# B and C of a scan step from one narrow matmul, spread over the partitions through DRAM

## What is computed

```python
dbc = xs @ x_proj_w.T                       # 16 columns for dt, 16 for B, 16 for C
dt = softplus(dbc[..., :16] @ dt_proj_w.T + dt_proj_b)
Bm = dbc[..., 16:32]
Cm = dbc[..., 32:]
dA = exp(dt[..., None] * A)
dBu = dt[..., None] * Bm[:, :, None, :] * xs[..., None]
hs = scan(h = dA * h + dBu)                 # along the tokens
y = einsum('blds,bls->bld', hs, Cm) + xs * Dvec
y = (y * silu(z)) @ out_proj_w.T
```

## Time and profile before

| | |
|---|---|
| median of 3 runs | 4836.43 us |
| the profiled execution's own time | 4842.17 us |
| its span, first to last instruction | 4840.4 us |
| mean granted TensorE clock | 0.957 of full speed |
| busy, of the span | PE 88%, DVE 83%, POOL 81%, ACT 68% |
| DMA | 623 MB, 129 GB/s on average |

### The profile page before, as it was taken

How to read it: one execution, slowest core, us unless ns; L and a number is a source line. 1 busy time by engine, 2 the same in 40 slices (tenths; PEclk the granted TensorE clock), 3 DMA queues, 4 the chain that set the end, 5 groups by cost and what they waited for, 6 DMA issues and landing times.

```text
span 4840.4 us, 69756 instructions
## 1 busy us (share of the span) xinstructions
PE 4236.6 (88%) x21206; PEld 1773.4 (37%) x21206; DVE 4002.3 (83%) x5617; ACT 3314.4 (68%) x5382; POOL 3939.5 (81%) x5162
## 2 busy tenths in 40 slices
PE   3578788999999999999989999999999989898897
PEld 1233333333333343434333434343333333333332
DVE  2268889888988888988898989888989898988872
ACT  1356566777777777777767776777777777676665
POOL 1268888888888888888888888888888889898873
PEclk9688899999999999999999999999999999999998
DMA  2366665656555665666656655666665665554430
GB/s 68 79 141 158 145 141 131 143 135 140 136 137 137 140 138 133 138 139 138 141 131 146 141 136 134 139 139 137 140 138 136 145 140 138 132 125 115 95 78 5
DMA packets 255529, 623.06 MB, mean 129 GB/s; under 512 B 105268, under 2 KB 170676, under 8 KB 255028
## 3 DMA queue, kind: packets, MB, share of 16 engines
q1 hardware_dynamic: 255156, 618.60, 55.8%
HBM read 540.85 MB, written 77.65 MB: 128 GB/s over the span
## 4 chain that ended last, share of the span: by engine, by line
POOL 35%; PE 24%; DVE 17%; issue 11%; DMA 7%; ACT 4%; SPq 0%; DVEq 0%; POOLq 0%; ACTq 0%
POOL hc L1156 14%; DVE hs L1011 7%; PE ps L676 5%; DMA dtb<-dt_scratch 5%; DVE ps L1001 4%; PE ps L740 3%; POOL sp L1169 2%; PE ps L689 2%; DVE tmpd L1070 2%; POOL h L1196 2%; POOL yw L1256 2%; PE ps L717 2%; POOL sp L1177 2%; PE ps L800 2%; PE ps L811 2%
## 5 line engine op out<-in xcount | busy, mean ns | idle before, releaser
L1156 POOL TENSOR_TENSOR hc<-hs,cb 128x448 f32<-128x448 f32 x1792 | 2025.6, 1137 | 460.5 <-DVE hs L1011 315.9
L1011 DVE TENSOR_TENSOR_SCAN hs<-dtb,state,ps 128x448 f32<-128x448 f32 x1536 | 1754.7, 1142 | 84.8 <-issue 0.7
L1001 DVE TENSOR_TENSOR ps<-ps,bb 128x448 f32<-128x448 f32 x1792 | 1099.1, 613 | 439.7 <-PE ps L676 437.9
L848 ACT ACTIVATE dtb<-dtb,decay 128x448 f32<-128x448 f32 x1792 | 1092.0, 658 | 156.0 <-DMA dtb<-dt_scratch 154.1
L676 PE MATMUL ps<-dux,pick 128*128 128x448 bf16 x3584 | 1038.1, 371 | 128.7 <-DVE hs L1011 117.1
L890 ACT ACTIVATE hg<-ps,be 128x448 f32<-128x448 f32 x896 | 523.8, 630 | 405.2 <-PE ps L740 404.6
L676 PE MATMUL ps<-duz,pick 128*128 128x448 bf16 x1792 | 642.5, 359 | 0.0
L676 PEld LDWEIGHTS ps<-dux,pick 128*128 128x128 bf16 x3584 | 283.7, 101 | 831.4 <-issue 432.1
L740 PE MATMUL ps<-xn,we 64*128 64x448 f32 x1792 | 564.5, 592 | 7.9 <-ACT hg L890 5.3
L879 ACT ACTIVATE rz<-ps,bnb 128x448 f32<-128x448 f32 x448 | 280.8, 627 | 271.4 <-PE ps L724 271.0
L689 PE MATMUL ps<-hc,gather 128*32 128x448 f32 x3584 | 451.3, 573 | 0.0
(11 more groups left out here) (171 smaller groups left out, 6319.3 us busy)
## 6 DMA issues: line engine op xcount, KB each, us to landing
dtb<-dt_scratch SPq DMA_DIRECT2D x448, 896.0 KB, 6.7
slab<-h_scratch SPq DMA_DIRECT2D x168, 290.0 KB, 8.3
dt_scratch<-sp SPq DMA_DIRECT2D x112, 224.0 KB, 2.0
h_scratch<-h2p SPq DMA_DIRECT2D x168, 112.0 KB
h<-h_scratch SPq DMA_DIRECT2D x56, 336.0 KB, 4.3
h_scratch<-h1s SPq DMA_DIRECT2D x56, 232.0 KB, 2.2
xw<-xn_scratch SPq DMA_DIRECT2D x112, 112.8 KB, 2.7
xw<-xn_scratch SPq DMA_DIRECT2D x112, 112.5 KB, 3.7
```

The costliest lines, as they stand in the source:

```text
L848: A.activation(a, a, ACT.Exp, scale=decay[k % 2][:, i:i + 1]).then_inc(a_ok, 1)
L1001: V.tensor_tensor(bank, bank, bb[:, k % 2, :], ALU.mult).then_inc(bu_ok, 1)
L1011: V.tensor_tensor_scan(rev(hs[:, n % RH, :], d), rev(dtb[i // 4][:, i % 4, :], d), rev(bank, d), state[:, d, i:i + 1] if k % STEPS >= 2 el ...
L1156: P_.tensor_tensor(hc[:, n % 8, :], hs[:, n % RH, :], cb[:, k % 2, :], ALU.mult).then_inc(hc_ok, 1)
```

## The change

Each step makes B and C together in one matmul with the plain weights of 32 columns, into 32 partitions (`bc` at slot -15). ACT copies 32 partitions (`copy_bc`). SP writes them to DRAM (`put_bc`, 56 KB) and reads them back twice with each row 8 times (`spread_b` and `spread_c`, 224 KB each), into the same double-buffered `bb` and `cb`. `weigh_b` and `by_c` now wait for these DMAs. `wbb` and `wcc` and the four DVE copies of the prologue that made them are gone. `AHEAD` goes from 6 to 5, and all place tables are new.

```diff
-AHEAD = 6
+AHEAD = 5
...
-STEP_AT = {'fetch_xw': -27, 'x': -20, 'silu_u': -20, 'dt': -17, 'soft_in': -17, 'bb': -12, 'copy_bb': -11, 'cc': -10, 'copy_cc': -9, 'z': -5, 'soft_le': -17, 'soft_ym': -17, 'soft_log': -15, 'soft_dt': -14, 'part0': -14, 'part1': -12, 'part2': -3, 'put_dt': -10, 'spread0': -5, 'spread1': -2, 'spread2': -2, 'spread3': 1, 'skip': 8, 'gather0': 9, 'gather1': 13, 'gather2': 15, 'gather3': 19, 'gate': 19, 'out_proj': 21, 'add_out': 21}
-UP_AT = (0, 0, 1, 1, 2, 2, 3, 3, 8, 8, 9, 9, 10, 10, 11, 11)
-DOWN_AT = (5, 7, 12, 15)
-PAIR_AT = (3, 7, 12, 14)
-THIRD_AT = (0, 0, 1, 2, 2, 3, 5, 5, 6, 7, 7, 10, 10, 11, 12, 13)
-FOLD_AT = (3, 5, 6, 8, 9, 11, 14, 14, 14)
-A_AT = {'cut': -11, 'second': -11, 'put0': -9, 'rem1': -9, 'split1': -7, 'put1': -6, 'rem2': -8, 'split2': -6, 'put2': -4, 'arrange': -1, 'x_in': 12, 'paths': 15, 'mean': 16, 'square': 18, 'var': 18, 'power': 18, 'scaled': 21, 'normed': 22, 'norm_T': 25, 'keep_xn': 26}
-F_AT = {'fetch': 1, 'x_T': 3, 'paths_in': 5, 'rows': 8}
-E_AT = {'mean': 1, 'square': 2, 'var': 2, 'power': 4, 'normed': 4, 'tokens_T': 9, 'logits': 10, 'compare': 12, 'places': 13, 'lead': 13, 'ask': 16, 'weigh': 19, 'share': 19, 'weights': 21, 'weight_parts': 21, 'parts': 25, 'fold': 49, 'out': 53}
+STEP_AT = {'fetch_xw': -22, 'x': -20, 'silu_u': -20, 'dt': -17, 'soft_in': -17, 'bc': -15, 'copy_bc': -14, 'put_bc': -11, 'spread_b': -6, 'spread_c': 0, 'z': -5, 'soft_le': -17, 'soft_ym': -16, 'soft_log': -14, 'soft_dt': -13, 'part0': -9, 'part1': -3, 'part2': -3, 'put_dt': -10, 'spread0': -6, 'spread1': -4, 'spread2': 0, 'spread3': 1, 'skip': 7, 'gather0': 8, 'gather1': 13, 'gather2': 15, 'gather3': 19, 'gate': 19, 'out_proj': 20, 'add_out': 20}
+UP_AT = (0, 0, 1, 1, 2, 2, 3, 3, 8, 8, 9, 9, 10, 10, 10, 10)
+DOWN_AT = (4, 7, 12, 15)
+PAIR_AT = (4, 6, 11, 12)
+THIRD_AT = (0, 0, 1, 2, 2, 3, 5, 5, 6, 7, 7, 9, 11, 12, 13, 13)
+FOLD_AT = (4, 6, 7, 8, 10, 10, 13, 14, 14)
+A_AT = {'cut': -16, 'second': -10, 'put0': -9, 'rem1': -9, 'split1': -7, 'put1': -5, 'rem2': -7, 'split2': -5, 'put2': -3, 'arrange': 0, 'x_in': 8, 'paths': 14, 'mean': 16, 'square': 18, 'var': 18, 'power': 19, 'scaled': 21, 'normed': 23, 'norm_T': 26, 'keep_xn': 27}
+F_AT = {'fetch': 1, 'x_T': 5, 'paths_in': 6, 'rows': 8}
+E_AT = {'mean': 0, 'square': 2, 'var': 2, 'power': 4, 'normed': 4, 'tokens_T': 9, 'logits': 10, 'compare': 12, 'places': 13, 'lead': 13, 'ask': 16, 'weigh': 18, 'share': 19, 'weights': 20, 'weight_parts': 22, 'parts': 25, 'fold': 47, 'out': 48}
...
+                def put_bc(kk):
+                    sp_.wait_ge(m_act, by_act("bc", kk))
+                    sp_.dma_start(bc_dram[kk % 2], bc[:, :]).then_inc(bc_out, 16)
+
+                def spread_bc(kk, half):
+                    sp_.wait_ge(bc_out, 16 * (kk + 1))
+                    if kk >= 2:
+                        sp_.wait_ge(hc_ok if half else bu_ok, DS * (kk - 1))
+                    out, landed = ((bb, bb_in), (cb, cb_in))[half]
+                    src = bc_dram[kk % 2, DS * half:DS * half + DS, :]
+                    sp_.dma_start(out[:, kk % 2, :], src.unsqueeze(1).to_broadcast([DS, 8, CH]))\
+                       .then_inc(landed[kk % 2], 16)
...
-                    if what == "bb":
-                        last = MM(out[:, 0:CH], wbb[of % 2][:, :], u[:, of % 2, :], start=True, stop=True)
-                    elif what == "cc":
-                        last = MM(out[:, 0:CH], wcc[of % 2][:, :], u[:, of % 2, :], start=True, stop=True)
+                    if what == "bc":
+                        last = MM(out[0:2 * DS, 0:CH], wbc[of % 2][:, :], u[:, of % 2, :], start=True, stop=True)
...
+                def copy_bc(kk):
+                    act.wait_ge(m_ps, misc_made("bc", kk))
+                    after(bc_out, 16 * kk)
+                    A.activation(bc[:, :], ps[MB][0:2 * DS, 0:CH], ACT.Copy).then_inc(m_act, 1)
...
-                        dve.wait_ge(m_act, by_act("bb", k))
+                        dve.wait_ge(bb_in[k % 2], 16 * (k // 2 + 1))
...
-                        pool.wait_ge(m_act, by_act("cc", k))
+                        pool.wait_ge(cb_in[k % 2], 16 * (k // 2 + 1))
```

More of the change, by code:

```diff
@@ L116, in build @@
         wdt = [sb(f"wdt{d}", [DI, DI]) for d in range(2)]
-        wbb = [sb(f"wbb{d}", [DI, 128]) for d in range(2)]
-        wcc = [sb(f"wcc{d}", [DI, 128]) for d in range(2)]
+        wbc = [sb(f"wbc{d}", [DI, 2 * DS]) for d in range(2)]
         skip = [sb(f"skip{d}", [DI, 128]) for d in range(2)]
@@ L143, in build @@
         dtb = [sb(f"dtb{j}", [128, 4, CH]) for j in range(4)]
+        bc = sb("bc", [2 * DS, CH])
         bb = sb("bb", [128, 2, CH])
@@ L193, in build @@
         rows = [early[:, 1408 + 128 * d:1536 + 128 * d] for d in range(2)]
-        wbc = [early[:, 1664 + 2 * DS * d:1664 + 2 * DS * d + 2 * DS] for d in range(2)]
         bnv = early[:, 1728:1810]
@@ L295, in _ @@
                                   dvec[d][:, 3:3 + DS].unsqueeze(2).to_broadcast([DI, DS, 8])).then_inc(s_rows, 1)
-                    for out, at in ((wbb[d], 0), (wcc[d], DS)):
-                        then(V.tensor_copy(out[:, :].rearrange("p (s e) -> p s e", e=8),
-                                           wbc[d][:, at:at + DS].unsqueeze(2).to_broadcast([DI, DS, 8])))
                     then(V.tensor_copy(wz[d][:, :].rearrange("p (q r) -> p q r", q=4),
@@ L378, in build @@
         xw_in = [sem("xw_in0"), sem("xw_in1")]
+        bc_out, bb_in, cb_in = sem("bc_out"), [sem("bb_in0"), sem("bb_in1")], [sem("cb_in0"), sem("cb_in1")]
         dtb_in = [sem(f"dtb_in{j}") for j in range(4)]
@@ L506, in build @@
         for k in range(LAST):
-            MISC += [(DS * k + STEP_AT[what], what, k) for what in ("x", "dt", "bb", "cc")]
+            MISC += [(DS * k + STEP_AT[what], what, k) for what in ("x", "dt", "bc")]
         for what in ("tokens_T", "logits", "fold"):
@@ L627, in _ @@
                         fetch_xw(kk)
+                    for kk in steps_at(n, "put_bc"):
+                        put_bc(kk)
+                    for kk in steps_at(n, "spread_b"):
+                        spread_bc(kk, 0)
+                    for kk in steps_at(n, "spread_c"):
+                        spread_bc(kk, 1)
                     for kk in steps_at(n, "put_dt"):
@@ L915, in soft_in @@
                     A.activation(sp[:, 2, :], sp[:, 0, :], ACT.Ln, bias=1.0).then_inc(dt_l, 1)
[L917 to L920, removed]
-                    A.activation(bb[:, kk % 2, :], ps[MB][:, 0:CH], ACT.Copy).then_inc(m_act, 1)
-                def copy_cc(kk):
-                    act.wait_ge(m_ps, misc_made("cc", kk))
-                    if kk >= 2:
-                        act.wait_ge(hc_ok, DS * (kk - 1))
-                    A.activation(cb[:, kk % 2, :], ps[MB][:, 0:CH], ACT.Copy).then_inc(m_act, 1)
+                def copy_bc(kk):
+                    act.wait_ge(m_ps, misc_made("bc", kk))
+                    after(bc_out, 16 * kk)
+                    A.activation(bc[:, :], ps[MB][0:2 * DS, 0:CH], ACT.Copy).then_inc(m_act, 1)
                 def split_h2(it, a):
@@ L973, in _ @@
                         weigh(it)
-                    for kk in steps_at(n, "copy_bb"):
-                        copy_bb(kk)
-                    for kk in steps_at(n, "copy_cc"):
-                        copy_cc(kk)
+                    for kk in steps_at(n, "copy_bc"):
+                        copy_bc(kk)
                     for kk in steps_at(n, "soft_in"):
```

1 line of the change is left out of this document (added).

## The result

The changed kernel takes 5140.06 us (median of 4 runs, 5122.29 to 5154.96), against 4834.59 us before on the same chip: a ratio of 1.0627 [1.0598, 1.0656], 305 us **slower**. 4782 us were forecast, with a range up to 4890. The worst rival stood at 4900. The profiled run took 5155 us, 15 above the median, at a mean granted clock of 0.923 (before: 0.957).

The account below looks back on a forecast made before the run. No engine alone was the bound: POOL set the pace in half a pair, the PE-DVE loop in the other, plus dtb[0]'s load. 76 + 22 - 24 - 20 = 54 us less gave 4782 us, range 4710 to 4890.

Parts of the forecast that it names:

- worst rival: The load of dtb[0] becomes the bound and is on the chain in every pair: 4900 us, 36% chance.
- Term (7): PE's bank MB: bc two slots behind the fold may wait for DVE's finish; 0 counted, 91 us kept for the range.
- Term (1): One f32 matmul per step removed from PE: 76 us gained, bounds 0 and 145.6.
- POOL and DVE keep the pace: Rival: PE's saving becomes idle time before L676 and terms (2) to (4) cancel; 4836 us, no change, 16% chance.
- Term (2): On POOL, part0 leaves the stretch without pauses and part1 changes ends: 22 us gained, bounds 0 and 64.
- Term (3): SP's queue: fetch_xw and spread_b ahead of the dtb[0] load lengthen ACT's wait; 24 us lost, bounds 0 and 123.
- 36% rival: The load of dtb[0] becomes the bound, on the chain in every pair: 4900 us, half of it 4868.
- Term (4): SP's arrange loads start 1.3 us later, so PE's third convolution waits for h: 20 us lost, bounds 0 and 73.
- Term (5): spread_c, behind put0 in SP's queue, may bring C late to POOL: 0 counted, bound 112 us.
- Term (6): In a pair's first step cut_slab precedes dtb[0], landing 6.7 us later; a margin of some 12 us holds: 0.
- Term (8): AHEAD 5 shortens ACT's lead before the scans: 0 taken, 34 us lost kept for the range.
- What would show it: Signs to check: L762's records gone, pair from 80.3 to 79.4 us, L848 waiting about 3.5 us, new waits per term.

Follow-up runs that it names:

- E14: The changed kernel with bc three slots later (-12), copy_bc, put_bc and spread_b later too, fold left alone: 5011.18 us, ratio 1.0339.
- E15: E14 with the experts' fold and the output projection a slot later and out back at 53: 4949.99 us, ratio 1.0213.
- E8: The kernel before with only the new tables of the convolution and the experts, STEP_AT and AHEAD as before: 5032.11 us, ratio 1.0390.
- E10: The kernel before with only the convolution's new tables (A_AT, F_AT, THIRD_AT, FOLD_AT): 5165.77 us, ratio 1.0662.
- E11: The kernel before with only the experts' new tables (E_AT, UP_AT, DOWN_AT, PAIR_AT): 5186.65 us, ratio 1.0702.
- E17: The kernel before with C's matmul and copy left out, by_c multiplying by B's tile, so its output differs: 4844.84 us, ratio 1.0016.
- E7: The kernel before with only the new STEP_AT and AHEAD 5, B and C at their old places: 4995.17 us, ratio 1.0330.
- E2: The code of before (two matmuls, no DRAM) with all new places and AHEAD 5: 5178.52 us, ratio 1.0696.
- E1: The new code with the places and AHEAD of before, put_bc standing ahead of put_dt: 5021.38 us, ratio 1.0371.
- E16: E15 with UP_AT as before and spread_c earlier, at -2: 4972.38 us, ratio 1.0261.
- E12: The kernel before with only AHEAD changed from 6 to 5: 4813.11 us, ratio 0.9934.
- E5: E1 with put_bc moved behind the dtb[0] load and spread_b one slot later: 4841.22 us, ratio 0.9999.

## Why the prediction was wrong

**Term (7), the step that failed by most.** I saw the row (18 waits, 42.4 us) and the two slots for three, and worked out 91 us if PE waits in all pairs. Then I counted 0, since "`pick_du` may run three slots ahead of the scan". The runs show the reverse: PE ran ahead, and so arrived while DVE was late. It waited in 50 pairs for 3.9 us, 194 us for the bound's 38 x 2.4 + 42.4 = 133. Undone (E14) it gave back 129 us, above the bound of 91. The bound was too small because I priced the new waits by the mean of the old ones, 2.4 us where they took 3.9. What the stretch at the 1.2 GHz level behind each wait adds is not separated: 129 us is less than the 152 us by which the wait itself had grown. The other 61 us that came back (E15) hang on places for which the sum had no term, and 110 us stay open.

**Terms not seen.** The fold and the output projection, a slot or two earlier, got no term. They wait 1.2 us or so for `soft_in` and `gate` in nearly every pair, and taking them back, together with `out`, is worth 61 us (E15). The other places got none either. E8, E10 and E11, on the old code, show that each set costs 3.9 to 7.0%. The prediction treated a place as free unless a wait was known at its target. In a program where each engine runs in order, an earlier place is a new chance to wait.

**Term (1), 76 us gained.** Its bounds were 0 and 145.6, and the truth was the lower end. E17 removes that matmul, its copy and all of C's path: 1.0016. Weighting by the chain's 52% was the error. Here the shares of the chain said who ended last in one execution, not what a shorter job yields where three engines stand at 87 to 92% in a loop. The rival "POOL and DVE keep the pace" had this part right: the wait before L676 grew from 117.1 to 141.9 us in E17.

**Term (2), 22 gained,** wasn't tried alone. E7, which has it with the rest of the step table, is 3.3% slower, and its trace shows a cost that the term left out. `part1` now stands right ahead of the third `part` on POOL, and PE waits for the latter once per pair (E7's list; 6.9 us in 6 places before):

```profile
PE ps L676 <- POOL duz L1189: 62.4, 54, 2.6
```

**Term (3), 24 lost, and the 36% rival.** The tile did come later after `put_dt`, by 1.8 us for the forecast 2.2, but not for the reason given. The median over all 448 `dtb` loads went from 6.7 us to 8.6. Yet the load that the term is about, `dtb[0]` of a pair's second step, needed 8.4 us from issue to landing before and 8.5 after (medians over steps 20 to 89). What grew is the time from `put_dt` to its issue, 1.96 us before and 3.70 after, since SP issues `fetch_xw` and `spread_b` in between. The bytes of these transfers, which stood ahead of the load, did not lengthen its landing measurably. I had priced the bytes, and laid the three issues beside the queue's backlog. SP after, and ACT's wait for the tile:

```profile
2131.07 0.34 SPq L537 DMA_DIRECT2D dt_scratch<-sp  x1
2131.51 1.30 SPq L620 DMA_DIRECT2D h<-h_scratch  x3
2132.91 1.11 SPq L572 DMA_DIRECT2D xw<-xn_scratch  x2
2134.12 0.55 SPq L557 DMA_DIRECT2D bb<-bc_scratch  x1
...
2143.18 0.67 ACT L863 ACTIVATE dtb<-dtb,decay 128x448 f32<-128x448 f32 x1 [1.80 <-DMA dtb<-dt_scratch]
```

The Trainium skill (DMA: Bandwidth & Descriptors, Anatomy of one DMA) gives its 2.0 us and 436e3 bytes per us for a transfer that GpSimd issues, while these are issued by SP. Worked out from it, 896 KB would take about 4.1 us, an estimate. This case's loads took 8.4 and 8.5 us from issue to landing, and the measurement decides. ACT's wait was 169.3 / 64 = 2.6 us each, not 3.5, and E2 is 7.0% slower with 64.3 us of it. So the rival's mechanism was not the loss, although its sign was right.

**Term (4), 20 lost.** L741 waited for `h` 11 times only, 85.3 us, up to 15.9 each and not once per pair. The mechanism was right in kind. It shows where PE is not held up elsewhere first: E7 has 54 such waits and 84.0 us against 11 and 52.6 before, 0.7 us for each new one, as forecast. In E1, where something else holds `arrange`, it is 56 waits and 200.8 us. (The rows gave 22.76 - 22.0 = 0.76 us of cover, not 0.6, which makes the term 16 us.)

**Term (5), 0.** POOL never waited for `cb`, though its load has 2% of the chain (the page's chain by line), and its earlier issue in E16 gained nothing. Right, as far as it goes. **Term (6), 0:** not tried alone, but the trace bears it out. In a pair's first step the tile lands 14.8 us after `put_dt` for 8.8 before (medians over the same steps), 6.0 later for the forecast 6.4, and the median of ACT's wait for it is 0.

**Term (8), 0 with a bound of 34 lost,** had the wrong sign. `AHEAD` 5 gains 0.66% (E12). Term (3) had credited it with 2.5 us per pair, but only against the new delay. That it would help by itself, 115 us less of waiting on ACT for 31 us of time, I did not ask.

**What would show it.** L762's records are gone, the wait for `finish` grew from 42.4 us to 194.4, and the pair moved to 85.8 us, not 79.4. The text named that wait as the sign of term (7), so the sign was read rightly and its weight wrongly.

## What to carry to other kernels

Where each engine takes its jobs in order and is busy some 90% of the time, ask of every job that moves earlier what its engine does if the input is not there yet. `bc` three slots later gave back 129 us, while the matmul that was saved was worth nothing. Price a new wait by how late the engine waited for is at that place, not by the mean of the waits of today: 3.9 us where the mean was 2.4. Judge a set of places as a set, since here each half of one cost more than the whole. In a queue with one order, a DMA that waits for its data belongs behind all that don't need it: E1 to E5 is 180 us. And look in the queue's own waits after each edit, since E14 and E15 brought in a new one of 7 us per step.

## What was not expected of the hardware

- A wait of PE of 4 us was followed by 6 us at a granted clock of 0.50, in which the f32 matmul of `bc` took 1.67 us, against 0.91 for `dt` at 2156.10 at full clock. The clock also fell with no such wait before it: PE was busy 1.57 and 1.48 us of the 2 us windows from 2142 and 2144 us, its longest hole 0.95 us, and was at 0.50 from 2146 to 2152. After the hole of 1.25 us before 2158.27 it stayed at 1.00.
- A write of 56 KB issued 0.6 us behind a load of 896 KB landed only 6.4 us later (E5, where the median of this write is 6.5). In the changed kernel, which issues it in another place, the same write has a median of 3.0 us, and `put_dt`'s 224 KB have 1.9.
